# An expert layer behind gated attention, with its routing planned in two parts

## What is computed

```python
# attention: 8 heads of 16, keys and values from ctx_2048 (256 wide)
x = x + jnp.tanh(g_xattn[0]) * xattn(ctx_2048, layernorm(x))
xf = layernorm(x).reshape(-1, 128)                  # 4096 tokens
probs = softmax(xf @ router_w.T)
topv, topi = jax.lax.top_k(probs, 2)
topv = topv / (topv.sum(-1, keepdims=True) + 1e-9)
cw = (one_hot(topi, 8) * topv[..., None]).sum(1)
h = gelu(einsum('td,edh->teh', xf, w1))             # 128 -> 512
y = einsum('teh,ehd->ted', h, w2)                   # 512 -> 128
x = x + jnp.tanh(g_ffn[0]) * einsum('te,ted->td', cw, y)
```

## Time and profile before

| | us |
|---|---|
| median of 3 runs | 447.86 |
| lowest and highest run | 447.83, 449.24 |
| the profiled execution | 445.81 |
| its span, first to last instruction | 444.0 |
| TensorE busy in the span | 348.9 |
| GpSimd busy | 257.4 |
| VectorE busy | 221.6 |
| ScalarE busy | 173.4 |

### The profile page before, as it was taken

The page is one execution under the profiler, slowest core; times in us unless marked ns, Lnnn a source line. Parts: engine busy times, 40 slices in busy tenths (PEclk is TensorE's granted clock), DMA queues, the critical chain, the costliest instruction groups (busy, mean ns, idle before and its releaser), DMA issues.

```text
span 444.0 us, 9908 instructions
## 1 busy us (share of the span) xinstructions
PE 348.9 (79%) x2947; PEld 285.2 (64%) x2948; DVE 221.6 (50%) x853; ACT 173.4 (39%) x410; POOL 257.4 (58%) x341
## 2 busy tenths in 40 slices
PE   0699999998999999999744006998898898899800
PEld 0466666676776667666534006898898898898800
DVE  1435345768768687867646351333333333333245
ACT  2144554545455554544420202443343343344300
POOL 2436364553587987868676771565565665665700
PEclk9999999999899999999965556999999999999965
DMA  6203340201012111551111132222221212222079
GB/s 206 72 25 119 120 120 26 71 26 61 25 48 85 44 55 33 147 139 37 32 42 37 48 97 50 66 55 61 71 57 55 71 54 62 58 64 66 23 248 319
DMA packets 41011, 34.36 MB, mean 77 GB/s; under 512 B 4964, under 2 KB 36870, under 8 KB 40976
## 3 DMA queue, kind: packets, MB, share of 16 engines
q1 hardware_dynamic: 32432, 23.36, 18.6%
q0 software_dynamic: 4320, 8.47, 5.7%
q10 hardware_dynamic: 4224, 2.10, 1.6%
HBM read 22.35 MB, written 12.01 MB: 77 GB/s over the span
## 4 chain that ended last, share of the span: by engine, by line
PE 63%; issue 14%; DVE 9%; DMA 5%; SPq 4%; POOL 4%; ACT 1%; another core or an unknown queue 0%; DVEq 0%; POOLq 0%
PE ps_ts L1184 15%; PE ps_o L1196 7%; PE ps_proj L1196 7%; PE ps_st L1033 5%; PE ps_st L1036 5%; PE ps_o L1124 3%; PE ps_proj L1080 3%; DVE x2n L951 2%; PE ps_ts L1050 2%; DMA maskbc<-picked 2%; PE ps_proj L1084 2%; PE ps_tail L1102 2%; PE ps_ts L1054 2%; DVE tw L811 2%; PE ps_tail L1111 2%
## 5 line engine op out<-in xcount | busy, mean ns | idle before, releaser
L563 POOL DMA_INDIRECT picked<-yo,xg x71 | 70.6, 995 | 11.8 <-POOL pscratch L554 11.6
L1184 PE MATMUL ps_ts<-xt,w1c 128*128 128x128 f32 x568 | 76.7, 279 | 0.0
L531 POOL DMA_INDIRECT rows<-xr,posi x64 | 63.6, 994 | 16.1 <-issue 15.5
L1184 PEld LDWEIGHTS ps_ts<-xt,w1c 128*128 128x128 f32 x568 | 70.3, 195 | 0.0
L505 POOL TENSOR_TENSOR kblk<-kT,headcol 128x512 fp32r<-128x512 f32 x32 | 33.3, 1040 | 53.4 <-ACT kT L615 53.3
L675 ACT ACTIVATE probT<-ps_ts 128x512 f32<-128x512 f32 x71 | 42.4, 597 | 46.3 <-PE ps_ts L1184 46.3
L904 DVE TENSOR_REDUCE rowmax<-ps_ts 128x8 fp32r<-128x1024 f32 x32 | 39.1, 1221 | 37.8 <-PE ps_ts L1054 37.8
L554 POOL TENSOR_TENSOR pscratch<-minus_half 1x1 f32<-1x1 f32 x95 | 23.9, 251 | 57.4 <-DVE yo L997 55.2
L1036 PEld LDWEIGHTS ps_st<-negident,rowmax 128*128 128x128 f32 x256 | 30.9, 189 | 24.6 <-issue 24.6
L602 ACT ACTIVATE probT<-ps_st,pencol 128x1024 f32<-128x1024 f32 x32 | 35.6, 1113 | 28.3 <-PE ps_st L1036 28.2
L989 DVE COPY w1c<-w1s 128x512 f32 x71 | 31.4, 443 | 19.1 <-PE ps_ts L1184 10.2
(11 more groups left out here) (137 smaller groups left out, 615.9 us busy)
## 6 DMA issues: line engine op xcount, KB each, us to landing
xg<-rows SPq DMA_DIRECT2D x71, 65.0 KB, 1.9
ctxs<-ctxT SPq DMA_DIRECT2D x32, 128.0 KB, 2.0
xs<-x SPq DMA_DIRECT2D x8, 256.0 KB
w1s<-w SPq DMA_DIRECT2D x4, 512.0 KB, 3.5
w2s<-w SPq DMA_DIRECT2D x8, 256.0 KB
w1s<-picked SPq DMA_DIRECT2D x4, 512.0 KB, 5.6
maskbc<-picked SPq DMA_DIRECT2D x4, 512.0 KB, 9.8
out<-xs ACTq DMA_DIRECT2D x8, 256.0 KB, 6.5
```

The lines of the kernel that those rows point to most:

```text
L531: nc.gpsimd.indirect_dma_start(out=rows, out_offset=bass.IndirectOffsetOnAxis(ap=posi[:, i, pick, b:b + 1], axis=0), in_=xr[:, i, pick, b, ...
L563: nc.gpsimd.indirect_dma_start(out=picked, out_offset=bass.IndirectOffsetOnAxis(ap=xg[:, r, D + 1:D + 2].bitcast(I32), axis=0), in_=yo[:, ...
L1184: last = nc.tensor.matmul(ps_score[i][:, c * 128:(c + 1) * 128], w1c[:, i, c * 128:(c + 1) * 128], xt[:, (r - LAG_UP) % XRING, :], start=T ...
```

## The change

The groups are cut in two parts, 0 to 5 (part A) and 6 and 7 (part B), and each part has its own counts, its own piece of every expert's region, its own pads and its own plan. Part A has 48 + 7 = 55 slots, part B 16 + 7 = 23, together 78.

The slots begin after pass 10. The steps of passes 11 and 12 are put between the slots of part A, one step ahead of every three slots, on every engine. The plan of part A stands in (10, 1), that of part B in (12, 3), ahead of the slots 21 to 23. All slots are written out; there is no loop. The results of part A are gathered, added and stored during the slots of part B; only the two groups of part B are left for the end. SyncE writes the pads of part B between the loads of slots 46 and 47. The gathers go into buffers that the attention no longer needs, since w1s stays in use. The exponential of the router in (11, 2) now stands between Gelus of the slots, so ScalarE loads the exponential's table and then Gelu's again there.

```diff
+GROUPS_A = 6
+PARTS = (range(0, GROUPS_A), range(GROUPS_A, GROUPS))
+TAIL = GROUPS_A + LAG_SEND
-SLOTS = PICKS // 128 + EXPERTS - 1
+SPARE = EXPERTS - 1
+SLOTS_OF = tuple(len(p) * GROUP * T * 2 // 128 + SPARE for p in PARTS)
+SLOTS = sum(SLOTS_OF)
+SLOTS_A = SLOTS_OF[0]
+PER = 3
+ADD_FROM = SLOTS_A + 11
...
-    for g in range(DRAINED):
+    for g in range(TAIL):
         for k in range(GROUP):
             body(g, k)
+def each_slot(step, slot):
+    j = 0
+    for g in range(TAIL, DRAINED):
+        for k in range(GROUP):
+            step(g, k)
+            for j in range(j, j + PER):
+                slot(j)
+            j += 1
+    for j in range(j, SLOTS + LAG_DOWN):
+        slot(j)
...
+            def pads(part):
+                sp.wait_ge(s_plan, PLAN * part + PAD_ROWS)
+                for e in range(EXPERTS):
+                    r = row_of(pad_row[0:1, part, e:e + 1], EXPERTS * REGION - 128)
+                    sp.dma_start(rows[bass.ds(r, 128), :], padrow[:, :]).then_inc(s_pads, 16)
+            def scattered(part):
+                sp.wait_ge(s_plan, PLAN * part + PLAN)
+                sp.wait_ge(s_pads, 16 * (2 + EXPERTS * (part + 1)))
+                for G in PARTS[part][-2:]:
+                    i, used = outbox(G)
+                    sp.wait_ge(s_send[i], SEND * (used + 1))
...
+            pads(0)
+            scattered(0)
+            for j in range(SLOTS_A - RING):
+                load(j)
+            pads(1)
+            for j in range(SLOTS_A - RING, SLOTS_A):
+                load(j)
+            scattered(1)
+            for j in range(SLOTS_A, SLOTS_A + RING):
+                load(j)
+            for G in PARTS[0]:
+                gather(G)
+                load(SLOTS_A + RING + G)
+            for j in range(SLOTS_A + RING + GROUPS_A, SLOTS):
+                load(j)
...
# VectorE, in step
+                if (g, k) == (TAIL - 1, 1):
+                    plan(0)
+                    nc.vector.memset(before[:, :], 0.0).then_inc(s_reset, 1)
+                if (g, k) == (DRAINED - 1, 3):
+                    plan(1)
# VectorE, at the end of a slot
+                G, second = divmod(n - ADD_FROM, 2)
+                if G in PARTS[0]:
+                    add(G, second)
...
# ScalarE, at the end of a slot
+                G, late = divmod(n - ADD_FROM - 3, 2)
+                if G in PARTS[0] and not late:
+                    store(G)
...
# TensorE, at the end of a step
+                if (g, k) == (TAIL - 1, 1):
+                    pe.wait_ge(s_pos, POS * GROUPS_A)
+                    pe.wait_ge(s_xnT, BATCH)
+                    nc.tensor.matmul(ps_xT[:, 0:EXPERTS], ones_b[:, :], before[:, :], start=True,
+                                     stop=True).then_inc(s_total, 1)
+                if (g, k) == (DRAINED - 1, 2):
+                    pe.wait_ge(s_pos, POS * GROUPS)
+                    nc.tensor.matmul(ps_tail[:, 0:EXPERTS], ones_b[:, :], before[:, :], start=True,
+                                     stop=True).then_inc(s_total, 1)
```

More of the change, by code:

```diff
@@ L1009, in _ @@
+            each_slot(step, slot)
+            for G in PARTS[1]:
+                add(G, 0)
+                add(G, 1)
         @block.tensor
```

276 lines of the change are left out of this document (132 added, 144 removed).

## The result

In the series on record the changed kernel takes 451.19 us in the median (447.53 to 452.77, 18 runs) and the kernel before 447.85 (445.57 to 449.24, 18 runs). The ratio is 1.0062, 95% interval 1.0046 to 1.0079. The time lies in the forecast range of 438.5 to 453.5; the direction is wrong. The profiled span goes from 444.0 to 448.3, by +4.3 where the sum of the prediction was -2.1. That the time is in the range is luck: the steps between the slots cost 13.5 us more than forecast and left their own range of 4 to 15, while the gaps, the pads and the front together came out 7.2 better.

What follows compares the result with a forecast made beforehand. TensorE's pace was taken to bound the slots, with the stretches ahead and behind exposed; seven terms sum to -2.1 us, own time 443.7, on the median of 447.86 giving 445.8 us, range 438.5 to 453.5.

Steps and rivals of the forecast that it cites:

- the steps between the slots: Steps of passes 11 and 12 among part A's slots: TensorE's own work and its waits add 7.0 us (4 to 15).
- the gaps: TensorE's register-load waits between turns of eight slots: nine written-out ones replace eight, -1.4 us (0 to -2.5).
- the pads: Part B's eight pads between loads of slots 46 and 47: TensorE waits 5.8 us (0.5 to 8) at slot 47.
- the front: Stretch before the first slot: it starts at 253.4 instead of 270.24 us, -16.8 us (-19 to -14).
- the router's product: In step (11, 2) on TensorE: as large as half a slot, 0.9 us.
- (11, 3): Step among the slots: TensorE waits for the chosen experts and does its products, sum 1.3 us.
- The first rival: Part B's pads are cheap, 0.65 us each, so TensorE waits 0.5 at slot 47: 440.5 us; chance 0.25.
- The tail: Behind the last slot: only two groups left to gather and add, -10.9 us (-9 to -11.5).
- the early gathers: Part A's gathers and stores beside slots 59 to 79: loads come later, +1.0 us (0 to 8).
- The second rival: GpSimd becomes the bound in the steps, its group sends added in full: 455.5 us; chance 0.11.
- The table loads: ScalarE's two in (11, 2): cost TensorE nothing; with the skill's drain the sum would be about 1.8 us higher.
- rivals 2 and 3: GpSimd bounds the steps (455.5 us); loads wait behind gathers in one queue (453.7 us); chance 0.11 each.

Runs made afterwards that it cites:

- c2_before_again: The kernel before, unaltered, run again as a kernel of its own for its trace: 444.02 us in one run, median of its series 442.89.
- e8_gathers_at_end: Changed kernel with the gathers, additions and stores of part A moved back behind the last slot: 447.34 us, ratio 1.0113 to the kernel before.
- e6_group5_first: Changed kernel with all eight sends of group 5 put ahead of rs2 of group 7: 433.80 us, ratio 0.9787 to the kernel before.
- c5_changed_fourth: The changed kernel unaltered, in a later series beside the kernel before: 437.11 us, ratio 0.9879.
- e3_sends_later: Changed kernel with the 16 sends of groups 6 and 7 one behind each send of slots 22 to 37: 449.31 us, ratio 1.0164 to before.
- e7_plan_pads_group5: Changed kernel with part B's plan one operation a slot, its pads one a load, group 5's sends ahead of rs2: 427.77 us, ratio 0.9671 to before.
- c1_changed_again: The changed kernel unaltered, in a later series beside the kernel before: 437.73 us, ratio 0.9882.
- e4_pads_spread: Changed kernel with part B's eight pads one behind each load of slots 39 to 46: 433.93 us, ratio 0.9808 to the kernel before.

## Why the prediction was wrong, point by point

**The steps between the slots, +7.0 (4 to 15): the step that failed.** On record they cost 20.5. The operations were sized well: the plan 4.8 us against 5.2, the router's product 0.9 against 0.9 (slot 6), (11, 3) 1.3 against 1.3, the table load for the exponential hidden. In the later series the term is 8.1, near the forecast, though its parts are not, so that this is in part luck: slot 23 with the plan of part B and the half clock 4.9 instead of 3.5, and nothing for GpSimd, since TensorE waits for no load there. What failed on record is the hand-over between engines. The prediction took it once, as a few tenths of a microsecond from rows of before, and moved chains that cross from TensorE to VectorE and ScalarE and back into a place where TensorE has 1.3 us to spare. In the series on record such a chain can be 1 to 3 us longer. Before the change these chains ran where TensorE was idle anyway, behind the last attention group. The change brings them into the slots, which makes them as dear as TensorE's own time; the late hand-overs and what follows them cost this kernel some 11 us, by its two traces. The profile of before had the sign, at 249.33, 250.76 and 253.64 above: idle times of 1 to 2 us behind operations that had ended. I had not asked what they would do in a slot. What makes a hand-over late stays open, as said above.

**The pads of part B, +5.8 (0.5 to 8):** too high, +3.8 on record and +3.0 later, because a pad costs 0.82 us and not 1.31. The 1.31 was read from one execution of before, in which the eight pads took 10.5 us; the same kernel took 6.67 in c2_before_again. The first rival had the mechanism right, and with 0.65 us its price too low. At 0.82 its sum, 0.33 + 8 x 0.82 + 0.9 - 1.9 - 4.0, gives 1.9, and TensorE waits 2.57.

**The gaps, -1.4 (0 to -2.5):** the direction was right, the size not. Most of the written-out gaps (slots 16, 32, 40, 56 and 64) show 0.49 to 0.66 us of idle time instead of the 1.01 of the earlier trace rows; this and the turns that are no longer a loop make the whole -5. Slot 72 has 1.25, of which the gathers are 0.5 (0.73 in e8_gathers_at_end). Why they are shorter than the written-out gap of before, no run asked.

**The front, -16.8:** -18.3. The chain is the predicted one link by link (plan, addition, rs2, last send, landing, load), and e6_group5_first shows it by cutting it. It is 1.5 shorter than forecast, 1.1 of it because the last send is only 5.5 and not 6.6 later. In the later series the term is -15.0, since the front of before is 3.8 shorter there without its late hand-overs. The prediction had the first load of before stand behind the pads. In c2_before_again the pads are over at 256.4 us, and the first load starts at 264.59, 2.6 behind the start of the last send (262.00); there it waits for the sends.

**The tail, -10.9, and the early gathers, +1.0:** right, both in the trace and by e8_gathers_at_end. On the rule from the Trainium skill weighed there, DMA: Bandwidth & Descriptors (Queues, rings and completion order): loads did stand behind gathers in one queue here, and it cost under 1 us in three of the four traces. In c5_changed_fourth, the fourth, it cost some 1.5: transposes waited 0.52 us for a load at slot 64 and 0.72 at slot 67. A load that waits for one gather is still in time; a pile of gathers ahead of a load does not arise, as SyncE issues one between two loads.

**The second rival** (GpSimd) is not what made the changed kernel slower: on record TensorE waits for no load between slots 1 and 47. But e3_sends_later and slot 24 of e7_plan_pads_group5 show its edge. **The table loads:** the drain of about 1.38 us beside a load that the Trainium skill states in ScalarE: Activation LUTs (What ACT_TABLE_LOAD costs) isn't seen, neither behind the load nor ahead of it; in c1_changed_again the operation before ends at 264.69, Gelu's table is loaded from 264.71 for 1.28 us and the Gelu starts at 266.00.

The chance of 0.30 for slower was put on rivals 2 and 3; the series on record went there by a cause that stood in neither of them.

## What to carry to other kernels

Moving a short chain of other engines from an idle stretch into a pipelined one makes each of its hand-overs part of the critical path; cost it with the longest hand-over that the trace shows anywhere, not with the usual one, and spread it one operation to a slot where the slack is. When a stall is taken out, look for who was catching up in it: here GpSimd's sends, so that a wait of 4.8 us taken out gave 1.6 to 2.8. A ratio from one series is a sample of one: 18 runs gave an interval of 1.0046 to 1.0079, and three later series of the same two kernels lie at 0.988. A price read in one trace is one too: the pads of before took 10.5 us in one trace and 6.67 in the next. Count the semaphore events when two traces of one kernel differ.

## What the runs showed of the hardware

**Late hand-overs.** In one series of five, both kernels show waits of 1 to 3 us between the end of an operation and the start of the one that it releases, on VectorE and ScalarE at the same moments. At lmax the semaphore's event itself came 1.49 us behind the product's end, against 0.01 in a later trace. The two traces of that series lack about three in ten semaphore events. The cause stays open.

**The clock behind a short stop.** TensorE's granted clock fell from 2.4 to 1.2 GHz behind stops of 3.87 and 4.29 us on record (products of eight in 2.00 and 2.05). Behind 3.99 us in c1_changed_again the first product still took 1.13 and the second 1.72. In e4_pads_spread, behind 3.89 us, no product was slow (1.13, 1.06, 1.06). At the pads nearly the same length of stop did both. Windows of the changed kernel on record, behind a stop of 2.57, and then of c1_changed_again, behind one of 2.62:

```profile
368.00:372.00 4.00, 3.85 (x23) 3.58 (x24) 0.83 (x2) 1.15 (x3) 0.65 (x2) 0.66 0.37 87
```

```profile
357.00:361.00 4.00, 3.22 (x29) 3.06 (x28) 0.83 (x2) 1.47 (x3) 1.18 (x2) 1.00 0.24 58
```

So the length of the stop alone does not tell whether the clock falls. The price is an estimate from the intervals. Slots 23 and 24 together take 8.74 us in e4_pads_spread, without a slow product, 9.6 in the three later traces of the changed kernel, and 10.6 in e6_group5_first: 0.9 to 1.9 us. At the pads it is 0.8, at slot 49.

**Indirect sends of two kinds by turns.** In e3_sends_later GpSimd needs 2.70 us for one of a slot and one of a group, 1.01 and 0.96 of them busy in the sends, the rest in small operations and idle pieces of 0.16 and 0.30 us ahead of them.
